# Early-fusion block: key features' high halves by a view, a reordered tokenizer head, and row statistics moved into the keys' loop

## What is computed

```python
# tokenizer: 512 image tokens a batch, then 128 text tokens
xb = 2 * pi * x[..., None] * freq_bands              # 6 bands
feat = concatenate([sin(xb), cos(xb)], -1).reshape(b, 512, -1)
h = concatenate([einsum('bnf,of->bno', feat, W), txt], 1)    # 8 x 640 x 192
# attention, 12 heads of 64, 4 query groups
x = layernorm(h)
k, v = x @ Wk, x @ Wv
q = layernorm(gelu((x @ Wq) @ Wt + bt)) * gt + betat
phi(t) = concatenate([relu(t), relu(-t)], -1)
kv = phi(k)^T v;  ksum = sum(phi(k))                 # per batch and head
out = phi(q) kv / (phi(q) . ksum)
h = h + gelu(layernorm(out @ Wf + bf)) @ Wo + bo
# soft mixture of 8 experts, 4 slots each
h = h + soft_experts(layernorm(h))
```

## Time and profile before

| | us |
|---|---|
| median of 3 runs (2595.62 to 2599.95) | 2598.04 |
| the profiled execution | 2596.41 |
| its span, first to last instruction | 2594.6 |
| mean granted TensorE clock | 0.966 |

### The profile page before, as it was taken

The page is one execution under the profiler, slowest core; times in us unless marked ns, Lnnn a source line. Parts: engine busy times, 40 slices in busy tenths (PEclk is TensorE's granted clock), DMA queues, the critical chain, the costliest instruction groups (busy, mean ns, idle before and its releaser), DMA issues. The chain is left out here.

```text
span 2594.6 us, 61547 instructions
## 1 busy us (share of the span) xinstructions
PE 2397.1 (92%) x21902; PEld 1695.1 (65%) x22138; DVE 2081.3 (80%) x3269; ACT 1849.9 (71%) x2910; POOL 1294.7 (50%) x1259
## 2 busy tenths in 40 slices
PE   3999999788879999999999999999999999999946
PEld 2777777555546666666666666666666666666634
DVE  6999999788877878787878787878778787878652
ACT  6676677455558777777777777777787877777741
POOL 0000000265556666666666666666666666666530
PEclk8999999899989999999999999999999999999965
DMA  7421120111100000000000000000000000000001
GB/s 141 119 53 39 36 55 18 46 44 36 36 19 2 1 0 0 0 0 0 0 0 0 0 0 0 0 0 0 0 0 0 0 0 0 0 0 0 1 7 61
DMA packets 39689, 46.28 MB, mean 18 GB/s; under 512 B 4096, under 2 KB 35840, under 8 KB 39320
## 3 DMA queue, kind: packets, MB, share of 16 engines
q1 hardware_dynamic: 38488, 45.11, 7.3%
q10 hardware_dynamic: 1152, 0.51, 0.1%
HBM read 41.67 MB, written 3.93 MB: 18 GB/s over the span
## 5 line engine op out<-in xcount | busy, mean ns | idle before, releaser
L996 ACT ACTIVATE phi<-ps_t,betat,gt 64x512 f32<-64x512 f32 (+1 forms) x1280 | 850.9, 665 | 17.1
L1200 POOL TENSOR_TENSOR phi_lo<-phi 128x512 bf16<-128x512 f32 x480 | 506.9, 1056 | 557.2 <-ACT phi L996 557.2
L923 PE MATMUL ps_y<-staging,o_hi 128*128 128x384 bf16 x1920 | 468.7, 326 | 20.1 <-DVE o_lo L1113 20.1
L923 PE MATMUL ps_y<-staging,o_lo 128*128 128x384 bf16 x1920 | 469.0, 326 | 0.0
L923 PE MATMUL ps_y<-wf_lo,o_hi 128*128 128x384 bf16 x1920 | 468.9, 326 | 0.0
L1192 POOL TENSOR_TENSOR q_ssq<-q_ssq,half 128x8 f32<-128x8 f32 x240 | 439.0, 1829 | 18.8
L1113 DVE TENSOR_TENSOR o_lo<-ps_u,o_hi 128x512 bf16<-128x512 f32 x240 | 164.5, 685 | 213.8 <-ACT o_hi L1006 213.8
L154 PE MATMUL acc<-w_b,feat 128*128 128x384 bf16 x1728 | 295.8, 331 | 42.7 <-DVE w_b L266 39.4
L1006 ACT ACTIVATE o_hi<-ps_u 128x512 bf16<-128x512 f32 x240 | 143.4, 598 | 241.2 <-PE ps_u L909 241.1
L154 PEld LDWEIGHTS acc<-w_b,feat 128*128 128x128 bf16 x1728 | 168.7, 99 | 158.2 <-DVE w_b L266 40.0
L923 PEld LDWEIGHTS ps_y<-staging,o_lo 128*128 128x128 bf16 x1920 | 187.8, 98 | 124.2
(11 more groups left out here) (214 smaller groups left out, 5457.0 us busy)
## 6 DMA issues: line engine op xcount, KB each, us to landing
xt<-in_x_dram SPq DMA_DIRECT2D x32, 320.0 KB, 5.6
wf_f<-in_wf_dram SPq DMA_DIRECT2D x24, 384.0 KB, 3.2
xt<-in_x_dram SPq DMA_DIRECT2D x32, 256.0 KB, 6.0
out_dram<-h SPq DMA_DIRECT2D x8, 480.0 KB, 4.6
staging<-in_wq_t_dram SPq DMA_DIRECT2D x1, 3072.0 KB, 10.7
staging<-in_tok_w_dram SPq DMA_DIRECT2D x12, 192.0 KB, 8.7
staging<-in_kv_w_dram SPq DMA_DIRECT2D x1, 1536.0 KB, 14.7
h<-in_tok_w_dram SPq DMA_DIRECT2D x6, 192.0 KB, 10.4
```

The source lines that it names most:

```text
L923: last = nc.tensor.matmul(ps_y[:, n, 0:HC], lhs, w[part][:, c, n * HC:(n + 1) * HC], start=c == 0 and lhs is oh and part == 'wf_hi', stop= ...
L996: last = nc.scalar.activation(phi[sign * DH:(sign + 1) * DH, j % 2, a:b, head, :], ps_t[rows, a * P:b * P].rearrange("p (i n) -> p i n", n ...
L1200: nc.gpsimd.tensor_tensor(phi_lo[:, j % 2, :, head], phi[:, j % 2, :, head], phi_hi[:, j % 2, :, head], ALU.subtract).then_inc(s["phi_lo_d ...
```

## The change

- Tokenizer: the slots of `x` and of the weights lie one after the other instead of alternating (one contiguous piece a partition); a pair's weights come in eight DMAs with a semaphore for sines and one for cosines, so they are split in two halves of nine slots, and PE may begin with the sines. The second half of the first batch's `x` is loaded ahead of the second and third pair of weights. The first batch takes its six steps in the order (half, pair) (0,0), (1,0), (0,1), (0,2), (1,1), (1,2). An activation of one column loads the sine table at the start. Batch 1 is written out instead of being in the loop.
- Weights: DVE takes the statistics of 10 tiles ahead of the products and none between them; POOL makes two roots of five tiles.
- Keys' loop: `kf` has four float32 buffers, `kf_hi` is a view of it (L633 is gone), the waits of ACT on DVE's and POOL's halves are replaced by one on `summed`. `store_kv(b - 1, 0)` and `(b - 1, 1)` stand between the two halves of tiles 0 and 1. In batches 0 to 5 each tile has one `bn_stats` ahead of its first half and one `bn_aggr` after its second, of the tile ten further on; POOL makes the roots after a batch's last tile, and DVE copies the ten values into `stats` at the start of the next batch. DVE's and POOL's last two batches are outside of the loop.
- Experts: two pairs of semaphores are merged.

```diff
@@ tokenizer
-                        sp.dma_start(xt[lanes, u, 0:NS:2, :], x[b, u, 0:TAIL, 0:FULL + 1]).then_inc(x_in[u], 16)
-                        sp.dma_start(xt[lanes, u, 1:NS:2, :], x[b, u, TAIL:P, 0:FULL]).then_inc(x_in[u], 16)
+                        sp.dma_start(xt[lanes, u, 0:FULL + 1, :], x[b, u, 0:TAIL, 0:FULL + 1]).then_inc(x_in[u], 16)
+                        sp.dma_start(xt[lanes, u, FULL + 1:NS, :], x[b, u, TAIL:P, 0:FULL]).then_inc(x_in[u], 16)
...
                 load_w(0)
+                load(0, 1)
                 load_w(1)
-                load(0, 1)
                 load_w(2)
+                for u in range(2):
+                    sp.wait_ge(reduced, ends(0, u))
+                    load(1, u)
...
+        FIRST = ((0, 0), (1, 0), (0, 1), (0, 2), (1, 1), (1, 2))
...
+                def waves(b, p):
+                    r = p % RING
+                    high_weights(b, p, 0)
+                    act.wait_ge(cos_ready, STEPS * b + p + 1)
                     nc.scalar.activation(feat[:, r, 0:NS], feat[:, r, 0:NS], ACT.Sin, scale=TWO_PI).then_inc(wave_ready, 1)
+                    high_weights(b, p, 1)
...
                 act.wait_ge(quarter_ready, 1)
+                nc.scalar.activation(warm[:, :], quarter[:, :], ACT.Sin)
@@ attention_weights
-                for k in range(2, TILES // PART):
-                    rstd(k)
...
-                for n in range(0, 8, 2):
+                for n in range(0, 2 * TPB, 2):
                     row_stats(n)
...
-                    if 8 + 2 * u < TILES:
-                        row_stats(8 + 2 * u)
@@ keys_and_values
-        kf = sb("kf", [P, 2, HH, 2, DH], F32)
-        kf_hi = sb("kf_hi", [P, 4, HH, 2, DH], BF16)
+        kf = sb("kf", [P, 4, HH, 2, DH], F32)
+        kf_hi = kf[:, :, :, :, :].bitcast(BF16)[:, :, :, :, 1::2]
...
-                    if not (early and t == 0):
-                        act.wait_ge(kf_hi_ready, 2 * n + hf - 1)
-                        act.wait_ge(kpos_lo_ready, 2 * n + hf - 1)
-                        act.wait_ge(kneg_lo_ready, 2 * n + hf - 1)
...
-                    nc.vector.tensor_copy(kf_hi[:, m], kf[:, hf]).then_inc(kf_hi_ready, 1)
-                    dve.wait_ge(kf_hi_ready, 2 * n + hf + 1)
...
+                    if not first and not last:
+                        dve.wait_ge(row_rstd, b)
+                        nc.vector.tensor_copy(stats[:, bass.ds(TPB * b + TPB, TPB), :], st[:, :, :]).then_inc(kept, 1)
                     for t in range(TPB):
                         n = TPB * b + t
+                        if ahead:
+                            if t == 0 and not first:
+                                dve.wait_ge(kept, b)
+                            nc.vector.bn_stats(bn[:, t, :], h[:, n + 2 * TPB, :]).then_inc(row_stat, 1)
                         halves(n, t, 0, first)
-                        if t == 1 and not first:
-                            store_kv(b - 1, 1)
+                        if t < 2 and not first:
+                            store_kv(b - 1, t)
+                        if ahead:
+                            dve.wait_ge(row_stat, n + 1)
                         halves(n, t, 1, first)
+                        if ahead:
+                            nc.vector.bn_aggr(st[:, t, :], bn[:, t, :]).then_inc(row_mean, 1)
                         if not (last and t >= TPB - 2):
                             low_x(n + 2, (t + 2) % TPB)
...
-                        if t == 0 and not first:
-                            store_kv(b - 1, 0)
...
+                def rstd(b):
+                    pool.wait_ge(row_mean, TPB * b + TPB)
+                    nc.gpsimd.tensor_tensor(st[:, :, 1], st[:, :, 1], w['eps'][:, 0:TPB], ALU.add).then_inc(row_var, 1)
+                    pool.wait_ge(row_var, b + 1)
+                    nc.gpsimd.tensor_tensor(st[:, :, 1], st[:, :, 1], w['half'][:, 0:TPB],
+                                            ALU.pow).then_inc(row_rstd, 1)
```

## The result

The kernel after takes 2557.12 us (median of 4 runs, 2556.21 to 2558.96) against 2597.54 us for the kernel before beside it (4 runs, 2595.62 to 2599.95): a ratio of 0.9845, 95% interval 0.9828 to 0.9862. The profiled execution took 2556.21 us with a span of 2554.4. The forecast was 2556.0.

A forecast was written before the change was run, and what follows sets the result against it. DVE was taken to bound the tokenizer; in the keys' loop, PE's pause for `store_kv` and the slower clock behind it were the largest excess. Gains 5.3 (head) + 5.5 (weights) + 31 (loop) = 42 us gave 2556 us, range 2537 to 2578.

The forecast's parts named there:

- The head: Tokenizer start: new order of loads and steps ends DVE's sixth low half at 89.2 instead of 94.57, gain 5.3 us.
- Rival (a): Head: data lands at 400 GB/s instead of 207, 5 us more gain, 2551 us; chance 0.15.
- The loop: Keys' loop: casts removed, statistics added, stores earlier; gain 24 in six periods, 2 in batch 0, 5 in batch 7, 31 us.
- PE's own work, 22.8: Steady batch of the keys' loop: five undisturbed tiles of 4.56 us of PE each, 22.8 us.
- `store_kv(1)`, 0.6 late: Tile 1 of a batch: the second store stays behind DVE's half and reaches PE 0.6 us late.
- The new wait, 1.5: Batch start: DVE's copy waits for POOL's root, so `v_lo` comes 1.0 or 1.8 us late; 1.5 taken.
- Three tiles with fusion weights, 1.2: Keys' loop: POOL's operations slow DVE and feed PE's accumulation just in time; 0.4 us a tile, 1.2 a batch.
- VectorE's tile falls to 3.8 us: Keys' loop: without casts, with statistics, DVE's tile falls from about 4.5 to 3.8 us, under PE's 4.56.
- (b): Keys' loop: the new wait takes the store's place and the clock falls; 16 us lost, 2572 us; chance 0.2.
- (c): Keys' loop runs at PE's pace: a batch of 24.0 us gives 13 us more, 2543 us; chance 0.12.
- (d): Keys' loop: POOL's port becomes the bound, the loop keeps its time, only head and weights gain; 2587 us; chance 0.05.
- (e): Keys' loop accumulation: strided view costs as a weight load, 64 us, slower than before at 2620 us; chance 0.03.

The follow-up runs named there:

- the version with 0.5 us of pauses: Kernel after, with the statistics back in the weights' stage and the second store at the end of tile 0: 2543.98 us, ratio 0.9796.
- the version with both moves: Kernel after, with VectorE's copy of the ten statistics behind the first half tile and the second store at the end of tile 0: 2548.56 us, ratio 0.982.

## Why the prediction was right, and where not

The total was right to about a microsecond, which is in part luck, since its terms were off in ways that cancel: 5.3 + 5.5 + 31 = 42 forecast; 7.7 + 6.2 + 28.1 less 1.8 in the attention, which the change doesn't touch, = 40.2 in the two spans.

*The head, 5.3 for 7.7.* The mechanism was right: the sixth low half was to end at 89.2 and ends at 86.6. Of the miss, 1.3 us is the data: the second `x` was put at 24.7 from 207 GB/s and came at 23.40. The rate went to 226 with the larger packets, and the run with the old slots has 24.61 and gives back 1.2 us. The chain of steps behind it was right to 0.3 (58.3 from 23.40 to 81.67; forecast 58.5, from 24.7 to 83.2), and the 1 us put on top for gaps and `add_h` did not come. Rival (a), the head at 400 GB/s, is wrong: the transfers, each to 64 partitions, the lower and the upper half in turn, stay near the 218 GB/s of the Trainium skill (SBUF — State Buffer, "Door 1: The DMA port swizzle"). The measured 226 is a little above it, and the step from 211 to 226 with the layout goes against the prediction's "the contiguous pieces bring nothing". No wait for the moved text tiles or later weights appeared.

*The weights, 5.5 for 6.2.* Within the range of 4.3 to 7.8. The run with all statistics in this stage confirms it on its own: 6.1. ACT's third and fourth long copies stop PE for 1.96 and 1.61 us (before 485.79 and 491.98), as forecast with about 2 each.

*The loop, 31 for 28.1.* The six periods gave 20.1 us for 24, the first batch 4.1 for 2, the last period and what follows it 4.0 for 5. A steady batch was forecast at 26.1 and takes 27.15. Term by term:
- PE's own work, 22.8, is 23.4 to 23.6: the step that took one undisturbed tile times five missed 0.12 to 0.16 us a tile. Even the version with 0.5 us of pauses has 23.65. This is 0.75 of the miss.
- `store_kv(1)`, 0.6 late, is 1.83 late: 1.23, the largest single part of the miss. The argument counted VectorE's instructions at their undisturbed durations. VectorE enters tile 1 late, because its two normalizations and its first low half stand beside four instructions of GpSimd and take 1.9 and 0.96 us instead of 0.7 and 0.55. With GpSimd's subtractions small the pause is 0.48.
- The new wait, 1.5, is 0.78: VectorE's wait of 0.59 and a held-up copy of 0.70 instead of 0.16. The hold-up was forecast as a possibility and is there (the copy at 610.21 ends at 610.91, GpSimd's instruction at 610.89), but the term was to be 1.0 without it and 1.8 with it.
- Three tiles with fusion weights, 1.2 beside the others, left 0.91 and 0.08 of visible pause; but the large subtractions for the fusion weights cost 1.9 us a batch in all pauses together, by the run that makes them small. The cost was put in the wrong place.

The sixth period, whose batch has no statistics any more, was forecast like the other five; it takes 24.3 (664.47 to 688.75 on ScalarE's stores), which gave back part of the miss.

What the forecast had wrong in kind is the step by which VectorE's tile falls to 3.8 us, under PE's 4.56, so that statistics in the loop cost only the new wait. The 3.8 holds for an undisturbed tile (577.11 to 582.46 less 1.62 us idle is 3.7), but over a whole batch VectorE is busy 23.28 us, 4.66 a tile, hardly under PE's 4.71, because stores, the copy and the held-up instructions come on top. Without the statistics it is 4.13 a tile, and they were not free even so. The statistics cost 2.3 us a batch, of which the wait is 0.8; the version with both moves and without any wait for the power still needs 25.6 where the same without statistics needs 24.1. In tiles 0 to 2 VectorE is late, by GpSimd's instructions and by its own: the 2.6 us that the statistics add to its busy time are paid with 2.3. The other way the exchange is poorer: the cast takes 5.2 us off VectorE's busy time in a batch and shortens the batch by 2.8 (27.60 to 24.83).

The early store was right in kind and depends on its company. Without statistics it takes 1.0 us of pause and 1.6 us of slow clock away. With them it only changes one pause of 2.03 for one of 1.83 in a steady batch, because with the late store that kernel keeps its clock too. The 1.6 us of clock in five of six batches were rightly booked with the store: with the cast and the early store the clock is at 1.00 in every batch (27.60), without the cast, with the late store and no statistics, it still falls in five of six.

The rivals: (b), the new wait taking the store's place with a slow clock, did not come, though the run with the copy moved shows it one step away. (c), a batch of 24.0, needs the statistics out of the loop and the second store moved: the version above reaches it at 24.1. (d) and (e) are wrong: the accumulation's matmuls on the strided view still follow each other at 0.03 us.

## What to carry to other kernels

Ask of each part of a change what it would do alone: this one is three gains and a loss, and its statistics should have stayed where they were. An engine whose mean load is below the bound's isn't free for that: look for the tiles in which its results come last, take its durations from the rows where its neighbour on the port is busy, and put new work elsewhere, or waits and stores that others need ahead of what can be blocked. Where a wait is taken away, look for the next pause and for the clock behind it before you book the gain.

## What the hardware showed that I had not expected

- The clock's fall isn't told by the length of the pause ahead of it. In the kernel before PE paused 2.7 us in each of six batches, and the clock fell in five (30.2 to 30.4 us) and not in the third (28.75). PE paused 1.83 in every steady batch of the kernel after and 2.03 in the one with the late store and the clock stayed at 2.4 GHz; it paused 1.95 and 2.17 in two others, and the projections behind it ran at 0.51 us (1.2 GHz) in some batches and 0.33 (2.4 GHz) in others of the same execution, with the same pauses around them. The two first projections behind the 1.95 in the run with the copy moved, in two neighbouring batches (from the timeline of PE):

```profile
564.45 0.51 PE L544 MATMUL ps_p<-shared,xh 128*128 128x384 bf16 x1
...
592.29 0.33 PE L544 MATMUL ps_p<-shared,xh 128*128 128x384 bf16 x1
```

  A fall costs 1.6 to 1.7 us each time. What decides between two such batches stays open.
- A GpSimd subtraction holds up also the normalization, an operation of VectorE with one tensor and two columns as operands (0.98 instead of 0.38), and a copy of ten values (0.70 instead of 0.16), as the Trainium skill's rule has it (SBUF — State Buffer, "Who interferes with whom"). `bn_stats` is never longer beside GpSimd: all 30 in the loop take 0.35 or 0.36. Nor does every GpSimd instruction hold VectorE up: beside the power over five columns (608.86, 1.17 us) the same normalization takes its undisturbed 0.38 and 0.31 (at 609.01 and 609.31), which the rule, as the prediction gives it, a lock held for the whole instruction, would not allow.
- Packets of 3 to 5 KB instead of 0.75 to 1 KB moved 226 instead of 211 GB/s, each transfer to 64 partitions.
